# Four queries of a batch in the middle thirds of the attention units, and the norm that feeds them one slot earlier

## The reference, cut to what matters

```python
q = jnp.einsum('bsd,hdk->bhsk', queries, Wq) + bq[None, :, None, :]
k = jnp.einsum('bsd,hdk->bhsk', keys, Wk) + bk[None, :, None, :]
v = jnp.einsum('bsd,hdk->bhsk', values, Wv) + bv[None, :, None, :]
scores = jnp.einsum('bhsk,bhtk->bhst', q, k) / jnp.sqrt(jnp.float32(HEAD_DIM))
probs = jax.nn.softmax(scores, axis=-1)
attended = jnp.einsum('bhst,bhtk->bhsk', probs, v)
```

## Time and profile before

| | before |
|---|---|
| median of 3 runs | 855.06 us |
| lowest and highest run | 848.70 and 855.27 us |
| the profiled execution | 855.58 us |
| its span, first to last instruction | 853.8 us |
| mean granted TensorE clock | 0.872 of 2.4 GHz |
| attention stage, `ots` copies of units 0 and 15 | 480.35 and 624.08 us |

### The profile page before, as it was taken

How to read it: one execution, slowest core, us unless ns; L and a number is a source line. 1 busy time by engine, 2 the same in 40 slices (tenths; PEclk the granted TensorE clock), 3 DMA queues, 4 the chain that set the end, 5 groups by cost and what they waited for, 6 DMA issues and landing times.

```text
span 853.8 us, 14392 instructions
## 1 busy us (share of the span) xinstructions
PE 638.7 (75%) x4127; PEld 416.8 (49%) x4155; DVE 588.3 (69%) x1604; ACT 428.3 (50%) x906; POOL 412.4 (48%) x436
## 2 busy tenths in 40 slices
PE   4598888887878879799995787787742224999991
PEld 1244334344334347669992443454421112888881
DVE  2766889889899865977775667968546666444443
ACT  2296886786879453464442363526331011555552
POOL 3316537378778263531555286758300002676741
PEclk9998999999989759999996999979975555999996
DMA  6587997565668225635766010100030000111115
GB/s 174 176 291 266 324 317 269 197 210 199 226 229 259 69 68 156 199 118 154 204 164 227 19 32 22 41 1 13 1 123 1 0 0 17 44 50 45 49 34 157
DMA packets 97477, 109.79 MB, mean 129 GB/s; under 512 B 12597, under 2 KB 80889, under 8 KB 97018
## 3 DMA queue, kind: packets, MB, share of 16 engines
q1 hardware_dynamic: 68986, 84.87, 30.5%
q0 software_dynamic: 6592, 13.51, 5.7%
q10 hardware_dynamic: 21824, 10.49, 4.3%
HBM read 84.38 MB, written 24.44 MB: 127 GB/s over the span
## 4 chain that ended last, share of the span: by engine, by line
PE 44%; DVE 28%; ACT 12%; issue 7%; DMA 4%; POOL 2%; SPq 2%; ACTq 1%; DVEq 0%; POOLq 0%
PE PS L2065 7%; PE PS L2282 4%; PE PS L2076 4%; DVE nmx L1570 3%; PE PS L2258 3%; PE PS L2263 3%; ACT oh L909 2%; DVE oh L1424 2%; PE PS L2273 2%; DMA oh<-index 2%; PE PS L2030 2%; PE PS L2187 2%; ACT gs L923 2%; PE PS L2158 2%; PE PS L2210 1%
## 5 line engine op out<-in xcount | busy, mean ns | idle before, releaser
L644 POOL DMA_INDIRECT xs<-xn,row x64 | 70.7, 1104 | 54.4 <-PE PS L2065 31.5
L693 POOL DMA_INDIRECT yb<-ys,yrow x64 | 62.1, 970 | 65.4 <-PE PS L2160 19.8
L780 POOL DMA_INDIRECT xg<-xrows,tok x39 | 37.5, 961 | 103.2 <-DVE tok L1771 91.6
L1990 PE MATMUL PS<-oh,T 128*128 128x512 bf16 x212 | 64.6, 409 | 16.9 <-ACT oh L910 14.4
L1424 DVE TENSOR_SCALAR oh<-oh,pcol 128x2048 bf16<-128x2048 bf16 x80 | 65.4, 818 | 16.5 <-DMA oh<-index 15.3
L2065 PE MATMUL PS<-xT,wgu 128*96 128x128 f32 x512 | 68.5, 278 | 5.1 <-issue 3.9
L1995 PE MATMUL PS<-oh,T 128*32 128x512 bf16 x960 | 71.5, 406 | 0.5 <-issue 0.4
L909 ACT ACTIVATE oh<-oh,pcol 128x512 bf16<-128x512 bf16 x80 | 57.8, 722 | 14.3 <-DMA oh<-index 14.3
L2065 PEld LDWEIGHTS PS<-xT,wgu 128*96 128x96 f32 x512 | 60.3, 166 | 7.6 <-issue 5.7
L2004 PE MATMUL PS<-ident,gs 128*128 128x128 f32 x320 | 54.4, 294 | 9.9 <-ACT vv L931 9.5
L910 ACT ACTIVATE oh<-oh,pcol 128x512 bf16<-128x512 bf16 x80 | 57.8, 722 | 2.6
(11 more groups left out here) (406 smaller groups left out, 1678.8 us busy)
## 6 DMA issues: line engine op xcount, KB each, us to landing
oh<-index SPq DMA_DIRECT2D x80, 512.0 KB, 3.6
oh<-index SPq DMA_DIRECT2D x80, 128.0 KB, 4.8
x<-xs SPq DMA_DIRECT2D x128, 64.0 KB
ys<-y ACTq DMA_DIRECT2D x64, 128.0 KB
w<-in_w SPq DMA_DIRECT2D x8, 384.0 KB, 5.6
xs<-nil SPq DMA_DIRECT2D x48, 64.0 KB
xs<-nil SPq DMA_DIRECT2D x7, 320.0 KB
wg1r<-in_wg SPq DMA_DIRECT2D x1, 2048.0 KB, 8.9
```

The costliest lines, as they stand in the source:

```text
L644: pool.indirect_dma_start(xs[:], bass.IndirectOffsetOnAxis(ap=row0[:, QT * b + t, k:k + 1], axis=0), xn1[:, b % 2, t, :], None).then_inc(s ...
L693: pool.indirect_dma_start(yb[:, b % 2, t, k, :], None, ys[b // 2][:], bass.IndirectOffsetOnAxis(ap=yrow0[:, QT * b + t, k:k + 1], axis=0))\
L1990: pe.matmul(o, T2[:, b % 2, p, n // NK, :], oh[:, slot, GH, :], start=(p == 0), stop=False, skip_group_check=True)
```

## The change

The queries of a batch move from q = -7, -5, -4, -2 (thirds 2, 1, 2, 1) to q = -8, -5, -2, 1 (all third 1), one in each of units 4b - 3, 4b - 2, 4b - 1 and 4b. Their additions on VectorE follow one slot behind, as before. The norm's statistics, deviation, apply, transposes and copy each move up one slot (q = -12, -11, -10, -9, -9), and GpSimd's gathers and adds for batches 2 and 3 as well, the gates of the gathers with them. The loop gets one slot more at the front. No instruction is added or removed.

```diff
 PERIOD = 3 * NG
-FRONT_FIRST, BACK_LAST = -11, 25
+FRONT_FIRST, BACK_LAST = -12, 25
 MAX_FIRST = -5
-GATHER_FIRST, ADD_FIRST = -22, -14
-Q_SLOTS = {-7: 0, -5: 1, -4: 2, -2: 3}
+GATHER_FIRST, ADD_FIRST = -23, -15
+Q_SLOTS = {-8: 0, -5: 1, -2: 2, 1: 3}
@@ SIDE
-        if _q == -8:
+        if _q == -9:
             SIDE["xn2T", _b, 0] = len(SIDE)
         if _q in Q_SLOTS:
             SIDE["q", _b, Q_SLOTS[_q]] = len(SIDE)
@@ ScalarE
-                    if q == -10:
+                    if q == -11:
                         deviation(NA, "0", B + b + 1)
-                    if q == -8:
+                    if q == -9:
                         act.wait_ge(s["side_ps"], SIDE["xn2T", b, 0] + 1)
                         act.copy(pnT[:], PS[:, 4, :]).then_inc(s["side_read"], 1)
@@ VectorE
-                    if q == -11:
+                    if q == -12:
                         dve.wait_ge(s["x2_ready"], b + 1)
                         norm_stats(c, NA, rows, "var0", QT - 1 if b == 0 else 0)
-                    if q == -9:
+                    if q == -10:
                         if b:
                             dve.wait_ge(s["side_read"], SIDE["xn2T", b - 1, 0] + 1)
                         norm_apply(NA, rows, xn2, "0", B + b + 1).then_inc(s["xn2_ready"], 1)
```

## The result

| | before | after |
|---|---|---|
| median, runs side by side on one chip | 853.18 us (20 runs, 846.15 to 857.00) | 858.26 us (20 runs, 852.73 to 866.48) |
| ratio, 95% interval | | 1.0083, 1.0060 to 1.0106 |
| the profiled execution | 855.58 us | 857.51 us |
| its span, mean granted TensorE clock | 853.8 us, 0.872 | 855.7 us, 0.864 |
| first copy of `pnT` to last copy of `ots` | 455.13 to 624.08, 169.0 us | 453.87 to 626.35, 172.5 us |

By the ratio the change makes the kernel slower by 0.8% of 853 us, 7.1 us (5.1 to 9.0); the two medians lie 5.1 us apart, at the low end of that. I go by ratios. From here on "the stage" is the stretch in the last line, from ScalarE's first L1042 to its last L1029. What follows the stage takes 229.3 to 230.0 us in every profile of this text but one; what precedes it varies from 451.4 to 460.2 us although no kernel here touches it.

The account below looks back on a forecast made before the run. No engine was taken as full: the stage alternates between VectorE and the round trip TensorE, ScalarE, TensorE. Terms -6.2 - 3.1 + 3.0 + 6.8 - 0.2 gave +0.3 on a median of 855.06, about 855.4 us, range 849 to 862.

Parts of the forecast that it names:

- bank 4 decides: Rival: TensorE waits in units 8 and 12 for VectorE's cost read, cools to 1.2 GHz; +4.5, 859.6 us; chance 0.22.
- Term 1: Units 2, 6, 10: first query leaves the last third, so the next scores start sooner after the output products; -6.2 us.
- Term 2: Units 3, 7, 11: third query leaves the last third, so VectorE's outputs and maximum start sooner; -3.1 us.
- Term 3: Units 1, 5, 9: norm's apply and transposes a slot earlier save nothing and delay the next maxima; +3.0 us.
- its sign in the trace: The idle before L2113 in unit 5 shrinking by a whole microsecond would show the forecast wrong.
- Term 4: Units 8 and 12: last query shares bank 4 with the router products, so TensorE waits for VectorE's read; +6.8 us.
- Term 5: Unit 7's L1127 mostly escapes GpSimd, but batch 3's statistics wait for L719 and unit 11 gets a collision; -0.2 us.
- The rival's threshold: Bank 4 was to decide once each wait in units 8 and 12 is longer than about 3 us.
- The third rival: VectorE, not ScalarE, ends the first- and third-query waits; their 9.3 us gain shrinks to 2; 862.7 us; chance 0.06.
- The fourth: Rival: L1127's collision with GpSimd goes and nothing comes back; 851.8 us; chance 0.1, counted in another rival's 0.22.

Follow-up runs that it names:

- e14: Kernel after with all four queries back in their slots of before, so only norm and gathers move up; ratio 1.0036.
- e1: Kernel after with the third and fourth query back at q = -4 and -2, so of the queries only the first moves; ratio 0.9972.
- e12: Kernel after with the third query at q = -3, right before the fourth, which is back at q = -2; ratio 0.9983.
- e8: Kernel after without GpSimd's weighing and summing of batch 3's gathered rows, only the last addition kept; less work; ratio 1.0039.
- e2: Kernel before with only its third and fourth query moved, to q = -2 and 1; ratio 1.0136.
- e3: Kernel after with the router products one slot earlier and VectorE reading them ahead of the norm statistics; ratio 1.0033.
- e11: Kernel after with the edits of e3 and e8 together, so less work; ratio 0.9952.
- e9: Kernel before without GpSimd's weighing and summing of batch 3's gathered rows, only the last addition kept; less work; ratio 1.0000.
- e4: Kernel after with GpSimd's gathers and adds of batches 2 and 3 another slot up; ratio 1.0127.
- e13: Kernel before again, one empty line added, for a second profile; ratio 0.9979.
- e10: Kernel after again, one empty line added, for a second profile; ratio 1.0105.

## Why the prediction was right or wrong

The time, 858.26 us, is 2.9 us over the forecast, inside the range, and the change is within 1%. That it is so near is luck: the kernel before came out at 853.18 in twenty runs where three had given 855.06. Nor was 1% the least that a measurement could tell from none, as I had written; the interval of 0.6 to 1.1% excludes no change. The change itself is +7.1 us, not +0.3, and that is the rival *bank 4 decides* (+4.5), which had 0.22. The ratios to the kernel before lay the change out in steps, each kernel against the one ahead of it: norm and gathers +3.1 (e14), the first query -5.5 (e1), the third query out of the last third +0.9, which is nothing (e12), the third and the fourth to their final places +8.5 (after). These sum to +7.0; each step has an error of some 4 us.

- **Term 1 (-6.2): right.** The seams are 1.63 us, as read off. Units 2, 6 and 10 together are 6.3 us shorter than in e14. One thing was missing: the query is on TensorE's path in the middle third too. I let it take the place of the transposes behind L2113 at no cost. From L2113 to the output products of unit 1 it was 1.4 us with the transposes between (before), 0.9 with nothing (e14) and 1.8 with the query (e1).
- **Term 2 (-3.1): right at its place, nothing as a step.** Units 3 and 7 went from 9.8 to 8.5, 1.25 and 1.2 as worked out. In unit 11, where I had 0.7, the two profiles of the kernel after differ by more than that (10.5 and 8.8, e1 10.4). But unit 4, where the fourth query now is, is 0.8 longer than in e1, and e12 shows that the gain depends on where the query goes.
- **Term 3 (+3.0): not refuted in sum, but its sign in the trace was badly chosen.** The idle before L2113 in unit 5, 2.42 us in the earlier trace rows, fell to 1.43, which I had named as proof against the term. The 1.0 that left it is found ahead of the transposes:

```profile
518.54 0.66 PE L2181 MATMUL PS<-ident,xn 128*128 128x128 f32 x4 [1.15 <-DVE att L1601]
521.38 1.09 PE L2113 MATMUL PS<-ident,NMp 128*128 128x128 f32 x4 [1.43 <-DVE NMp L1575]
```

  1.15 + 1.43 is as much idling as before; VectorE's unbroken run sets both. What counts is when L2113 starts after the last `ots` copy: 6.28 us before and 6.78 after in unit 1, 6.26 and 6.54 in unit 9 (I had 0.65 for each), 7.19 and 9.04 in unit 5. Of the 1.85 in unit 5, 1.55 stand already at the unit's first L2113, behind batch 2's statistics, which waited 1.06 us for L719 in unit 4. I had looked for that wait in batch 3 only. The sum agrees with e14's +3.1, whose interval is wide.
- **Term 4 (+6.8, bounds 5.5 and 9): right in kind, undersized, and its bound was too.** From the start of the router products to the end of the output products unit 8 took 5.5 us before and 15.9 after (+10.4 for 3.8), unit 12 took 3.4 and 7.9 (+4.5 for 3.0). In unit 12 the wait is 2.05 us as predicted (2.1), the query at full clock is the 0.9 of the sum, and the other 1.5 are the clock: the query took 2.08 and the scores 1.84 us instead of 1.02 and 0.72. I had put that case at the bound only. In unit 8 the 2.4 us of wait are 3.17 (e8), and 5.6 come on top from VectorE. In e2 term 4 stands nearly alone, and there too it is above its bound of 9: +11.6 us (6.8 to 16.4) with term 2's gain in it.
- **Term 5 (-0.2): the right two facts, in the wrong relation.** L1127 in unit 7 took 1.11 us and the statistics waited for L719, both as said. I netted them as a cap on a lead of 4.6 us, and charged term 4's wait as if the cap had been paid. But VectorE stands still ahead of L1653, with TensorE blocked behind that. The maxima, the output products and the query, which TensorE could do meanwhile, don't start. e3 and e8 each take one of the two away for 0.4 to 0.5%, e11 both for 1.3%. L1574 and L1575 after the wait, beside GpSimd's splits, took 1.61 us together instead of 0.72 in unit 8 before. Unit 11's L1127 met a split, as said, for 1.0 us and not 0.6:

```profile
586.97 2.08 DVE L1127 TENSOR_SCALAR xn<-XR,mvc,rstdc 128x128 f32<-128x128 f32 x4
```

- **The base.** The sum was made against one execution whose stage took 169.0 us. I corrected it to the median by its total, 0.5 us, which says nothing of the stage. The second profile has 164.8 at nearly the same total (854.46), and 3.6 us of the difference are unit 8 at a grant of 0.66. So my figures for the units next to it were those of a slow draw, and part of what term 4 would cost was already in the base.
- **The rival's threshold.** I wrote that bank 4 decides once *each* wait is longer than about 3 us. One wait of 8.75 and one of 2.05 decided it, and in e2 4.46 and 2.04.
- **The third rival** (VectorE ends the waits of terms 1 and 2, 862.7 us) is refuted by the seams and by units 3 and 7. **The fourth** (the collision goes, nothing comes back) is what e9 is for the kernel before: 1.0000, not -3.6 us.

What stays open: in e3 and e11 the profiled execution (849.58 and 842.65 us) was 4 and 6 us faster than the median of their runs (853.35 and 849.15), so their stages are low draws, and how far an average one is from them isn't known. No version was found that is surely faster than the kernel before with all work kept; e1 and e12 reach 0.9972 and 0.9983, with 1 in their intervals. Whether GpSimd's gathers can be placed so that its sums meet neither L1127 nor the statistics wasn't tried beyond e4.

## What to carry to other kernels

When a step is moved into a slot where its buffer is read by another engine's *last* instruction of that slot, price the new wait by everything that stands ahead of that instruction, waits of its own included: two waits in a row on two engines don't net against each other's lead. Before a gain of a few microseconds is weighed, take a second profile of the kernel before, and compare stage by stage; here one draw of the stage differed from another by 4.2 us at nearly equal totals. A gap removed at one place is worth what the next shared resource leaves of it, so run the move with the resource's other user out of its way (e3, e11) before judging the move.

## What the runs showed of the hardware

- Operations of 16 elements a partition on VectorE took 2.47 and 1.29 us beside GpSimd's L714 and L715, and 0.19 alone. Each ended about 0.05 us behind GpSimd's instruction, and the held-up ones of L1127 that come next ended 0.08 to 0.09 us behind it.
- Four short `tensor_scalar` (L1127, 1.11 us in all) took 5.53 to 6.73 us where GpSimd's train of multiplications and additions began 0.1 to 0.3 us behind them (before, e1, e4, e13), 6.54 and 5.60 where it began 0.11 and 1.04 us ahead (e12, e14), and 1.11 where it began 1.24 and 2.05 us behind (e2, after; the rows are those of the latter):

```profile
538.85 1.11 DVE L1127 TENSOR_SCALAR xn<-XR,mvc,rstdc 128x128 f32<-128x128 f32 x4
...
540.90 1.94 POOL L714 TENSOR_TENSOR yb<-yb,w0all 128x1024 f32<-128x1024 f32 x1 [2.41 <-DMA yb<-ys,yrow]
```

- The recorded starts don't show that the one to begin first goes first, as the prediction reads the row of unit 7: in e4 the first of the four L1127 began 0.09 us before L714 and still took 2.07 us, to 0.08 us behind its end.
- TensorE came back at 1.2 GHz after a wait of 2.05 us in unit 12 of the kernel after (L2135 1.84 us; mean grant 0.52 from 599.8 to 603 us). In e10 the first instructions after the same wait ran at 2.4 GHz, and the output products behind them at 1.2 (L2159 1.91 us). In the kernel before the grant in one and the same stretch was 0.66 in one execution and 0.89 in another.
